# Router matmuls between the transposes of the probabilities, and the low parts of the FFN weights on GpSimd, in a fused attention and mixture-of-experts kernel

## The reference, cut to what matters

```python
# x, ctx_2048: 64 sequences x 64 tokens x 256, float32
x = x + tanh(g_xattn) * xattn(layernorm(x), ctx_2048)      # q, k, v, RMS norm, rope, softmax, Wo
# 16 heads of 128, 4 key/value heads; keys are 64 of the context and 64 of x
y = layernorm(x)
probs = softmax(y @ w_router)                              # 8 experts
top_v, top_i = top_k(probs, 2); top_v = top_v / sum(top_v)
routed = sum over the two experts e of a token: top_v * 2.5 * (silu(y @ w_gate[e]) * (y @ w_up[e])) @ w_down[e]
shared = (silu(y @ ws_gate) * (y @ ws_up)) @ ws_down
x = x + tanh(g_ffn) * (routed + shared)
```

## Time and profile before

| | us |
|---|---|
| median of 3 runs | 1232.12 (1231.70 to 1232.45) |
| the profiled execution, its own time | 1231.9 |
| its span, first to last instruction | 1230.1 |
| granted clock of TensorE, as a share of full speed | 0.997 |
| attention stage, from the first matmul to the last pair's end | about 25 to 960 |

### The profile page before, as it was taken

The page is one execution under the profiler, slowest core; times in us unless marked ns, Lnnn a source line. Parts: engine busy times, 40 slices in busy tenths (PEclk is TensorE's granted clock), DMA queues, the critical chain, the costliest instruction groups (busy, mean ns, idle before and its releaser), DMA issues.

```text
span 1230.1 us, 31844 instructions
## 1 busy us (share of the span) xinstructions
PE 1204.1 (98%) x8909; PEld 1128.0 (92%) x8910; DVE 1034.9 (84%) x3026; ACT 905.3 (74%) x3786; POOL 936.2 (76%) x1124
## 2 busy tenths in 40 slices
PE   6899999999999999999999999999999999999998
PEld 3788899999999999999999999999999899999997
DVE  8788999999999999999999999988888677777443
ACT  7978788878887888788877888777777546666322
POOL 2778888888888888888888888888887425555664
PEclk9999999999999999999999999999999999999999
DMA  6634233322222323223333333222237536554574
GB/s 176 201 108 133 74 110 106 102 90 90 90 90 90 94 90 94 90 90 104 112 104 97 106 110 115 88 75 75 75 110 216 190 112 182 166 160 144 185 240 150
DMA packets 128792, 148.57 MB, mean 121 GB/s; under 512 B 13824, under 2 KB 108288, under 8 KB 127968
## 3 DMA queue, kind: packets, MB, share of 16 engines
q1 hardware_dynamic: 122256, 130.16, 35.0%
q0 software_dynamic: 6480, 17.77, 3.9%
HBM read 66.93 MB, written 80.76 MB: 120 GB/s over the span
## 4 chain that ended last, share of the span: by engine, by line
PE 91%; DVE 4%; ACT 3%; issue 1%; DMA 0%; SPq 0%; another core or an unknown queue 0%; ACTq 0%; DVEq 0%
PE b_kv L1733 14%; PE b_q L1719 13%; PE b_o L1817 13%; PE b_sc L1791 9%; PE b_aT L1806 9%; PE b_pT L1799 5%; PE b_qT L1780 4%; PE b_q L2053 3%; PE b_kv L2053 3%; PE b_q L1850 2%; PE b_kT L1776 2%; PE b_kT L1850 2%; PE b_aT L1968 1%; PE b_aT L2070 1%; PE b_pT L2070 1%; ACT probs L953 1%
## 5 line engine op out<-in xcount | busy, mean ns | idle before, releaser
L1733 PE MATMUL b_kv<-w_group,kv_in_hi 128*128 128x256 f32 x992 | 205.0, 304 | 0.0
L953 ACT ACTIVATE probs<-b_sc,neg_max 128x128 f32<-128x128 f32 x512 | 180.6, 371 | 2.6 <-DVE neg_max L1291 2.1
L747 POOL TENSOR_TENSOR q_rot<-q_rot,q_sin 128x512 f32<-128x512 f32 x128 | 176.7, 1381 | 7.5 <-DVE q_sin L1281 2.7
L743 POOL TENSOR_TENSOR qk_r<-qk_me,minus_half 128x6 f32<-128x6 f32 x128 | 171.8, 1342 | 10.1
L1733 PEld LDWEIGHTS b_kv<-w_group,kv_in_hi 128*128 128x128 f32 x992 | 161.4, 190 | 7.3 <-issue 0.4
L1719 PE MATMUL b_q<-w_group,kv_in_hi 128*128 128x512 f32 x496 | 164.8, 413 | 0.4 <-DVE q_sin L1281 0.4
L1817 PE MATMUL b_o<-wo_hi,aT_hi 128*128 128x256 f32 x480 | 143.5, 299 | 0.3 <-DVE aT_lo L1305 0.3
L1791 PE MATMUL b_sc<-kT,qT 128*128 128x128 f32 x1024 | 136.0, 276 | 6.2 <-ACT qT L942 4.4
L750 POOL TENSOR_TENSOR q_rot<-q_rot,qk_r 128x512 f32<-128x512 f32 x128 | 133.7, 1044 | 10.0
L1733 PE MATMUL b_kv<-w_group,kv_in_lo 128*128 128x256 f32 x496 | 139.7, 282 | 0.0
L936 ACT ACTIVATE junk<-b_q 128x128 bf16<-128x128 f32 x512 | 133.9, 283 | 0.0
(11 more groups left out here) (313 smaller groups left out, 3980.3 us busy)
## 6 DMA issues: line engine op xcount, KB each, us to landing
xs_scratch<-zeros SPq DMA_DIRECT2D x34, 1032.0 KB, 6.3
s_in<-xs_scratch SPq DMA_DIRECT2D x71, 129.0 KB
yT_scratch<-yT SPq DMA_DIRECT2D x32, 256.0 KB
yS<-yT_scratch SPq DMA_DIRECT2D x32, 256.0 KB
routed<-ys_scratch SPq DMA_DIRECT2D x32, 256.0 KB, 3.4
w_hi_all<-w_scratch SPq DMA_DIRECT2D x3, 1536.0 KB, 14.8
x_in<-in_x SPq DMA_DIRECT2D x32, 128.0 KB, 2.3
ctx_raw<-in_ctxT SPq DMA_DIRECT2D x32, 128.0 KB, 2.5
```

What stands on the lines that cost most here:

```text
L743: nc.gpsimd.tensor_tensor(qk_r[g % 2][:], qk_me[:], minus_half[:, 0:REP + NB], ALU.pow).then_inc(r_ready, 1)
L747: nc.gpsimd.tensor_tensor(q_rot[g % 2][:], q_rot[g % 2][:], q_sin[g % 2][:], ALU.add) \
L953: last = nc.scalar.activation(probs[:, j, :], b_sc[:, j * P:(j + 1) * P], ACT.Exp, bias=neg_max[g % 2][:, j:j + 1], accum_out=row_sum[g % ...
L1733: last = nc.tensor.matmul(b_kv[:, s * 2 * HD:(s + 1) * 2 * HD], kv_in[p][a][:, c, 2 * s:2 * s + 2, :], wkv_of(b, c)[:, g % KVH, :], start= ...
```

## The change

It has two parts. First, `probs_T` takes a function that it calls after two of its four transposes, and for g = 3 this function is the router; the call of the router behind `queries` is gone. Second, `piece_lo` moves from DVE to GpSimd. It now stands in unit g = 3 instead of g = 2, behind `key_sum(n + 1)`, and besides `w2_hi` (the high part is there) it waits for `p_normed2` of the unit (count 4t + 4), that is, for DVE's L1299. GpSimd's list is now written by `stretches` instead of `walk`, so that it knows the part.

```diff
 @block.gpsimd
+            def piece_lo(t, p, part):
+
+                pool.wait_ge(w2_hi, t - 1)
+                pool.wait_ge(p_normed2, 4 * t + 4)
+                raw, lo, wide = w2_piece(t, part)
+                nc.gpsimd.tensor_tensor(lo, raw, w2_new[p][:, 0:wide].bitcast(F32), ALU.subtract).then_inc(w2_lo, 1)
...
                         key_sum(n + 1, g + 1)
+                    if g == 3 and part is not None:
+                        piece_lo(t, p, part)
...
-            walk(pool, pair)
+            stretches(pool, pair)
 @block.vector
-            def piece_lo(t, p, part):
-
-                dve.wait_ge(w2_hi, t - 1)
-                raw, lo, wide = w2_piece(t, part)
-                nc.vector.tensor_tensor(lo, raw, w2_new[p][:, 0:wide].bitcast(F32), ALU.subtract).then_inc(w2_lo, 1)
...
-                    if g == 2 and part is not None:
-                        piece_lo(t, p, part)
 @block.tensor
-            def probs_T(n, g):
+            def probs_T(n, g, between=None):
...
                 for j in range(REP):
+                    if between is not None and j == REP // 2:
+                        between()
                     last = nc.tensor.transpose(b_pT[:, j * P:(j + 1) * P], probs[:, j, :], ident[:])
...
+                    between = None
+                    if g == 3 and not (first and p == 0):
+                        between = lambda: router(t - 1)
                     if not (first and u < 1):
-                        probs_T(n - 1, g - 1)
+                        probs_T(n - 1, g - 1, between)
...
-                    if g == 3 and not (first and p == 0):
-                        router(t - 1)
```

More of the change, by code:

```diff
@@ L777, in _, with pair @@
             key_sum(0, 0)
-            def pair(i, first, last):
+            def pair(i, first, last, part):
                 for u in range(2 * KVH):
```

## The result

The changed kernel takes 1245.0 us (median; 1244.5 to 1246.2), the kernel before 1232.1: 12.9 us more, a ratio of 1.0106 with a 95% interval of 1.0092 to 1.0120. The forecast was 1240.4 with a range to 1245.0. The direction and both places were right, the size was not: 12.9 us instead of 8.3.

A forecast was written before the change was run, and what follows sets the result against it. PE's own list in the attention stage was taken as the bound. Terms 3.5 - 0.1 + 0.1 + 1.5 + 1.7 + 1.8 gave 8.5 us over the profiled 1231.9: 1240.4 us, range 1233.5 to 1245.0.

The forecast's parts named there:

- The reading of the bound: Attention stage: PE busy 98% of the span, so nearly every change to its own list goes into the time.
- Part 1: Router between the transposes: waits for its late operand y_fine, net +0.12 us for each of 29 tiles, +3.5 in sum.
- The price of the place with the operand there: Router between transposes, operand ready: costs 0.24 us there, saves 0.31 behind `queries`, gain 0.07 a tile.
- The lengths of the piece: The piece as a GpSimd subtraction in unit 3: 1.13 us for 440 columns, 1.49 for 608.
- That the piece holds L1357: DVE's subtraction of the two logits (L1366 afterwards) is held by the piece, starting 0.28 or 0.64 us late.
- Rivals 1 and 2: First: y_fine precedes PE, L1357 not held, 1228.7 us, chance 0.05. Second: only the router's wait is felt, 1234.3, chance 0.17.
- Rival 3: The piece is late or long on GpSimd and everything behind L1357 moves with it: 1245 to 1248 us, chance 0.13.
- what hangs on the held subtraction: Late L1357 delays ACT's lead_tanh and PE's scores: 0.1 and 1.5 us with p = 0, 1.7 and 1.8 with p = 1.
- The slack of the p = 0 tiles: Between ACT's `queries_out` (L942) and PE's scores: 0.27 us, leaving 0.01 per 440-column piece, 0.37 per 608-column piece.
- The start of the piece: On GpSimd in unit 3, some 0.1 us behind DVE's L1299; 4.15 counts from the unit's first transpose load.
- The bounds: Router's wait +0.07 to +0.14 a tile; a piece starting 0.2 later or lasting 1.49 at 440 columns adds 5 to 8 us.

## Why the prediction was wrong

**What held.** The reading of the bound (PE's own list in the attention stage). Part 1 in full: +0.12 a tile, the router at +0.50, `queries` at +0.86 (forecast 0.87), the wait ended by y_bits, 3.6 us against 3.4, though 0.05 more in the p = 0 tiles with 440 columns. The price of the place with the operand there: 0.067 against 0.07. The lengths of the piece, 1.13 and 1.49, to the last digit. That the piece holds L1357 until 0.14 before its end: L1366 ends within 0.02 us of the piece's end. (That GpSimd's work on two tensors from SBUF holds DVE, as the prediction put it in general, is too wide: L743 does not.) Rivals 1 and 2 are out: 9.5 us of wait, and 508 ns. Rival 3 is right in direction: the piece came later than I took it.

**What failed** is the size of what hangs on the held subtraction, 9.1 us instead of 5.1, in three terms; the second, the start of the piece on GpSimd, is the largest.

1. *The slack of the p = 0 tiles*, "0.27", from which 0.01 was left for each piece of 440 columns. I had read 0.31 from L942's end to the scores' load in a tile where PE did not wait, and took 0.04 off for the wait, for which I named no row; it is the size of other pairs of engines (DVE to ACT 0.04 in the earlier trace rows, DVE to PE 0.05 in the earlier trace rows). ACT to PE it is more, as tile 14 of the changed kernel shows, where PE does wait:

```profile
482.04 0.60 ACT L951 ACTIVATE qT<-b_qT 128x512 f32<-128x512 f32 x1
482.75 0.74 PEld L1792 LDWEIGHTS b_sc<-kT,qT 128*128 128x128 f32 x6
```

0.11 us from 482.64 to 482.75. The slack was 0.20. That is 0.07 for each of 13 pieces, 0.9 us.

2. *The start of the piece*, forecast at 4.15, with 0.1 for the wait behind L1299. It was 4.24, and 4.29 in the p = 0 tiles with 440 columns: L1308 ends at 4.04, as forecast, but GpSimd starts 0.2 later. In those tiles the router's unit is 0.05 longer too, which takes the 0.05 off again. Against PE, `lead_tanh` was 0.36 and 0.73 us late instead of 0.28 and 0.64: 0.09 for 24 pieces, 2.2 us.

3. *One unit further.* I let the lateness end at the scores of the next unit. The unit after that is longer too: by 0.05 in the p = 0 tiles with 440 columns, by 0.09 in the p = 1 tiles with 608, and by 0.33 and 0.16 in two single units, of tiles 18 and 19. 1.2 us in sum.

The three make 4.3 us, against 4.0 that were missing; the p = 1 tiles with 440 columns gave 0.1 back.

The bounds had this partly: "if it begins 0.2 later" stood in the text, as rival 3 with 0.13. But I put only some 0.1 for the wait of GpSimd behind DVE. The trace of before had nearer rows. With several semaphores to wait for, GpSimd's L756 starts 0.14 behind DVE's L1267, as in tile 14, unit 1 (458.91 + 0.34 = 459.25, then 459.40; the record's ends are rounded):

```profile
458.91 0.34 DVE L1267 SCALAR_TENSOR_TENSOR k_sin<-b_kv,qk_r,sin_w 128x128 f32<-128x128 f32 x1
459.40 0.73 POOL L756 TENSOR_TENSOR k_rot<-k_rot,k_sin 128x256 f32<-128x256 f32 x1
```

The piece's own wait is 0.14 and 0.15 in tiles 3 and 2, which are written out, and 0.20 in the loops, so half of the missing 0.1 could have been read from the trace. The forecast should have stood in the middle of its bound.

## What to carry to other kernels

An instruction put into GpSimd's idle time is not free: ask which DVE instructions with two SBUF tensors start while it runs, or conversions and tensor_scalars with two columns, and who waits for them; a one-column subtraction with two operands from SBUF was worth 8.5 us here, and rewriting it with a scalar operand took that away. A matmul group moved to a cheaper place brings its price only if its operand is there; move the operand's producers first. When pricing a lateness, read the semaphore's cost from a row of that very pair of engines, with as many waits.

## What the runs showed of the hardware

- A two-column conversion on DVE (L1373), which reads one tensor, was held 1.33 us by a GpSimd subtraction; MAX8, a copy out of PSUM and a one-column tensor_scalar ran beside the same pieces in their usual time.
- GpSimd's L743, a power of six columns that takes 1.36 us, held neither an instruction with two tensors (0.16 us) nor a tensor_scalar with two columns (0.22). In the trace of before a tensor_scalar of 256 columns takes 0.40 us beside L743, 28 times, and 0.94 once, beside GpSimd's product L722.
- The wait across engines, from the end of one record to the start of the other: DVE to PE's loads 0.05, ACT to PE's loads 0.11, DVE to GpSimd 0.08 for one semaphore (L747), 0.14 for the piece's two in the written-out tile 3, and 0.20 for the same two in a loop, where the count and the address are computed.
- The second indirect DMA instruction of a tile takes 1.07 us on GpSimd, and 1.43 in six tiles of a loop in the runs with the piece as one instruction there, not with the piece on DVE or cut in two; unexplained.
